# Weights of the modulation first, zero products on TensorE, values in pairs, and another order of the last batch

## What is computed

```
mod = swish(c) @ w_mod + b_mod
sh_msa, sc_msa, g_msa, sh_mlp, sc_mlp, g_mlp = split(mod, 6)
xn = ln(x) * (1 + sc_msa) + sh_msa
q, k, v = heads(xn @ w_qkv + b_qkv)
q, k = ln(q, g_q), ln(k, g_k)
o = softmax(q @ k.T * HD ** -0.5) @ v
x = x + g_msa * (o @ w_proj + b_proj)
xn2 = ln(x) * (1 + sc_mlp) + sh_mlp
x = x + g_mlp * (gelu(xn2 @ w1 + b1) @ w2 + b2)
```

## Time and profile before

| what | value |
|---|---|
| median of 3 runs | 204.37 us (201.6 to 204.68) |
| the profiled execution's own time | 202.29 us |
| its span, first to last instruction | 200.5 us |
| mean granted clock of PE in it | 0.974 |
| PE busy | 166.0 us, 83% |
| DVE busy | 125.7 us, 63% |
| ACT busy | 108.9 us, 54% |
| POOL busy | 65.5 us, 33% |

### The profile page before, as it was taken

One profiled execution on the slowest core, in us unless ns is written; L12 is line 12 of the kernel. 1 busy time (PEld: TensorE's weight loads), 2 busy tenths in 40 slices (PEclk: granted clock), 3 DMA queues, 4 the chain that ended last, 5 costly groups with the idle time before them and its releaser, 6 DMA issues.

```text
span 200.5 us, 3873 instructions
## 1 busy us (share of the span) xinstructions
PE 166.0 (83%) x1504; PEld 93.9 (47%) x1504; DVE 125.7 (63%) x312; ACT 108.9 (54%) x146; POOL 65.5 (33%) x81
## 2 busy tenths in 40 slices
PE   0009982749979999999999999899659999999983
PEld 0005131413434454544644545344316796979773
DVE  3269568819548587679677774955856786564212
ACT  2001024255998879978888799976842404132320
POOL 8103513067418146173290201600462352220000
PEclk9999999999999999999999999999856999999999
DMA  0993028950000000000000000000000000101101
GB/s 10 247 211 120 5 51 251 399 158 0 3 2 0 3 3 0 0 3 0 3 0 5 0 3 2 0 3 0 3 0 0 0 3 0 60 3 59 59 0 59
DMA packets 4535, 8.67 MB, mean 43 GB/s; under 512 B 821, under 2 KB 3071, under 8 KB 4406
## 3 DMA queue, kind: packets, MB, share of 16 engines
q1 hardware_dynamic: 4228, 8.41, 14.0%
q10 hardware_dynamic: 288, 0.01, 0.1%
HBM read 7.21 MB, written 1.21 MB: 42 GB/s over the span
## 4 chain that ended last, share of the span: by engine, by line
PE 73%; DVE 9%; DMA 6%; ACT 3%; POOL 3%; issue 3%; SPq 1%; POOLq 0%; ACTq 0%
PE ps_o L1103 15%; PE ps_o L1226 10%; PE ps_s L1209 9%; PE ps_s L1088 8%; PE ps_x L1022 8%; DMA pTs<-in_b_mod 6%; PE ps_x L1029 4%; PE ps_o L1131 4%; PE ps_x L1113 4%; PE ps_s L1006 3%; PE ps_o L1015 3%; PE ps_x L1197 2%; PE ps_s L1000 2%; POOL z2s L464 2%; DVE kst L753 2%
## 5 line engine op out<-in xcount | busy, mean ns | idle before, releaser
L552 ACT ACTIVATE pTs<-ps_s,escale 128x1024 f32<-128x1024 f32 x64 | 68.9, 1109 | 17.1 <-PE ps_s L1088 16.1
L1103 PE MATMUL ps_o<-pTs,v 128*32 128x256 f32 x512 | 42.9, 410 | 5.0 <-ACT raw L523 2.5
L609 ACT ACTIVATE late<-ps_s 120x512 f32<-120x512 f32 (+1 forms) x20 | 11.9, 596 | 26.1 <-PE ps_s L1209 26.1
L1088 PE MATMUL ps_s<-qT,kT 32*128 32x256 f16 x256 | 24.3, 282 | 1.0 <-DVE qT L777 1.0
L1226 PE MATMUL ps_o<-w_sb,late 120*128 120x144 f32 (+1 forms) x160 | 20.7, 287 | 0.7 <-ACT late L609 0.7
L1226 PEld LDWEIGHTS ps_o<-w_sb,late 120*128 120x128 f32 (+1 forms) x160 | 19.9, 190 | 1.2 <-ACT late L609 1.2
L1209 PE MATMUL ps_s<-late,w1s 110*120 110x512 f16 (+1 forms) x80 | 18.8, 386 | 0.0
L1103 PEld LDWEIGHTS ps_o<-pTs,v 128*32 128x32 f32 x512 | 10.5, 110 | 17.5 <-ACT pTs L552 7.1
L1088 PEld LDWEIGHTS ps_s<-qT,kT 32*128 32x128 f16 x256 | 7.1, 93 | 24.4 <-issue 20.8
L464 POOL TENSOR_TENSOR z2s<-z2s,mbc 128x576 f32<-128x576 f32 x4 | 8.4, 2092 | 28.7 <-DVE z2s L901 28.7
L397 POOL COPY v<-raw 128x288 f32<-128x288 f32 x8 | 4.0, 496 | 41.8 <-DVE ssum L726 34.9
(11 more groups left out here) (115 smaller groups left out, 263.4 us busy)
## 6 DMA issues: line engine op xcount, KB each, us to landing
mbc<-mod_rows SPq DMA_DIRECT2D x6, 432.0 KB, 7.4
late<-in_w SPq DMA_DIRECT2D x1, 990.0 KB
xall<-in_x SPq DMA_DIRECT2D x1, 864.0 KB, 13.6
out<-late SPq DMA_DIRECT2D x3, 288.0 KB, 2.3
z2s<-in_w_qkv SPq DMA_DIRECT2D x1, 742.5 KB
mbc<-mod_rows SPq DMA_DIRECT2D x2, 288.0 KB, 6.4
pTs<-in_w_mod SPq DMA_DIRECT2D x1, 486.0 KB
w_sb<-in_w SPq DMA_DIRECT2D x1, 337.5 KB
```

What stands on the lines that cost most here:

```text
L552: nc.scalar.activation(pT[u % NP].rearrange("p g n -> p (g n)"), ps_s[:, 2 * (u % 2):2 * (u % 2) + 2, :].rearrange("p a n -> p (a n)"), AC ...
L609: nc.scalar.activation(hT[k % 2][0:FW[f], f, :], ps_s[0:FW[f], (NF * k + f) % 4, :], ACT.Gelu_apprx_tanh, scale=UNSCALE).then_inc(gelued, 1)
L1088: mm = nc.tensor.matmul(ps_s[:, 2 * (u % 2) + a, half * N:(half + 1) * N], kT[par][rows, j, i * P:(i + 1) * P], qT[par][rows, j, :], start ...
L1103: mm = nc.tensor.matmul(ps_o[SLOT * g:SLOT * (g + 1), 1, (j % 2) * N:(j % 2 + 1) * N], v[par][:, i, h, :], pT[u % NP][:, g, :], start=(i = ...
```

## The change

In the start SP loads `w_mod` and `b_mod` ahead of `w_qkv` and x, and the rest of x is issued only when the first x has landed. PE gets a buffer of zeros, `idle_z`, and multiplies it with itself, 128 by 128 by 512 in fp16, into a bank that isn't in use: 17 times before it waits for `w_mod`, 38 times before it waits for `wq`, and 2, 10 and 8 times within the preparation of batch 0. Their results are overwritten. DVE makes the constants of g first; the standardising and first modulating of batch 0 come before `wq`, in `xt`. `scores` 1 of batch 0 comes before `make_qkv(1)`.

In the loop PE takes values 0 and 1, 2 and 3, 4 and 5 in a row, each pair behind one more unit of scores. POOL splits w1 after batch 1's share, DVE in two halves at the end of batches 3 and 4.

The statistics' roots of batches 0 to 3 (tiles 0 to 7, `READY`) are taken in batch 6, so that the first pair's z is made there. In the last batch the z transposes of pair 0 and 1 go by halves through a bank of `ps_o`, the hidden products of pair 0 begin before values 7, and those of pair 1 before the output products of pair 0.

```diff
...
+        def z_bank(k, h):
+            return (x_bank if k < 2 else bank16(h)).rearrange("p c n -> p (c n)").rearrange("p (c n) -> p c n", c=2)
...
             xp = x.rearrange("b (p i) c -> p b (i c)", i=I)
-            sp.dma_start(xall[:, 0:2], xp[:, 0:2]).then_inc(ld_x, 16)
+            sp.dma_start(wm_sb[0:HT], w_mod).then_inc(ld_wm, 16)
+            sp.dma_start(wm_sb[HT:HT + 1, 0, :], b_mod.rearrange("(o c) -> o c", o=1)).then_inc(ld_wm, 16)
             sp.dma_start(wq_f, w_qkv).then_inc(ld_wq, 16)
             sp.dma_start(lo_row[:], lo_rows).then_inc(ld_wq, 16)
-            sp.dma_start(wm_sb[0:HT], w_mod).then_inc(ld_wm, 16)
-            sp.dma_start(wm_sb[HT:HT + 1, 0, :], b_mod.rearrange("(o c) -> o c", o=1)).then_inc(ld_wm, 16)
+            sp.dma_start(xall[:, 0:2], xp[:, 0:2]).then_inc(ld_x, 16)
             sp.dma_start(id32[:], ident).then_inc(ld_id, 16)
+            sp.wait_ge(ld_x, 16)
             sp.dma_start(xall[:, 2:B], xp[:, 2:B]).then_inc(ld_rest, 16)
...
+            pool.wait_ge(ld_w1, 16)
+            nc.gpsimd.tensor_scalar(w1_h, w1_f, WS, lo_row[:, 0:1], ALU.mult, ALU.mult).then_inc(w1_made, 1)
...
-            pool.wait_ge(ld_w1, 16)
-            nc.gpsimd.tensor_scalar(w1_h, w1_f, WS, lo_row[:, 0:1], ALU.mult, ALU.mult).then_inc(w1_made, 1)
...
-            x_roots(first_stats)
...
+            x_roots(first_stats)
...
                 exponentials(n, 3)
-                if not makes:
-                    early_roots()
+                if n == B - 2:
+                    early_roots(0, slice(0, READY))
                 exponentials(n, 4)
...
                 exponentials(n, 6)
+                if not makes:
+                    early_roots(1, slice(READY, EARLY))
                 exponentials(n, 7)
...
-            output(B - 1, 1, 1)
...
+                    if (k, f) == (0, 2):
+                        output(B - 1, 1, 1)
...
+            dve.wait_ge(ld_wq, 32)
+            wh = wq_f[:, :, 0:2 * H].rearrange("p c (h d) -> p c h d", d=HD)
+            nc.vector.tensor_reduce(wq_m[:], wh, AX.X, ALU.add).then_inc(D.sem, 1)
+            dve.wait_ge(ld_x, 16)
+            x_stats(first_stats)
+            x_aggregate(first_stats)
+            done("mean")
+            nc.vector.scalar_tensor_tensor(wh, wq_m[:].unsqueeze(3).broadcast_to([KR, NC, 2 * NH, HD]), -1.0 / HD, wh,
+                                           ALU.mult, ALU.add).then_inc(D.sem, 1)
+            x_newton(first_stats)
...
+            dve.wait_ge(first_stats.root.sem, first_stats.root.after(0, "rstd"))
+            for i in range(I):
+                nc.vector.tensor_scalar(xt[:, i, :], xi[:, i, :], mv[:, i, 0:1], rstd[:, i:i + 1],
+                                        ALU.subtract, ALU.mult).then_inc(prep.mx.sem, 1)
+            dve.wait_ge(set_act.sem, set_act.after(0, "A01"))
+            dve.wait_ge(prep.mx.sem, prep.mx.after(0, "z1"))
+            nc.vector.tensor_tensor(xt[:], xt[:], mb(0, A1), ALU.mult).then_inc(prep.mx.sem, 1)
+            def shift_first():
+                dve.wait_ge(prep.mx.sem, prep.mx.after(0, "za"))
+                nc.vector.tensor_tensor(xm[:], xt[:], mb(0, B1), ALU.add).then_inc(prep.mx.sem, 1)
...
+            def zT_half(k, h):
+                dve.wait_ge(ln2_pe.sem, ln2_pe.after(k, f"zT{h}"))
+                if k >= 2:
...
+                nc.vector.tensor_copy(zT[k % 2][:, 2 * h:2 * h + 2, :], z_bank(k, h)[0:KR]).then_inc(ln2_T.sem, 1)
+            def zT_out(k):
+                for h in range(2):
+                    zT_half(k, h)
...
+            def roots(part, tiles):
+                if part < 2:
+                    dve.wait_ge(root_act.sem, root_act.after(part, "y0"))
...
+            def first_half_z():
+                roots(0, ready)
+                standardise2(0)
+            def w1_half(c):
+                dve.wait_ge(w1_made, 1)
+                nc.vector.scalar_tensor_tensor(w1s[:, c:c + 2], w1_f[:, c:c + 2], WS, w1_h[:, c:c + 2],
+                                               ALU.mult, ALU.subtract).then_inc(w1_made, 1)
...
+                if n == B - 2:
+                    aggregate(ready)
...
                     xT_out(n + 2, prep)
+                if n == B - 2:
+                    first_half_z()
                 if n >= 2:
                     residual(n - 2)
+                if n in (3, 4):
+                    w1_half(2 * (n - 3))
...
                                             ).then_inc(fin_dve.sem, 1)
-            early, late_tiles = range(EARLY), range(EARLY, B * I)
             projected(B - 3)
             normalise(B - 2)
+            stack2(0)
             residual(B - 3)
+            channels(B - 2)
+            zT_half(0, 0)
+            standardise2(1)
+            zT_half(0, 1)
+            dve.wait_ge(w1_made, 3)
+            nc.vector.memset(hT[1][FW[-1]:FW[-1] + 1, NF - 1, :], 1.0).then_inc(h_ones, 1)
+            projected(B - 2)
             aggregate(early)
-            dve.wait_ge(root_act.sem, root_act.after(0, "y0"))
-            roots(0, early)
-            standardise2(0)
-            channels(B - 2)
-            dve.wait_ge(w1_made, 1)
-            nc.vector.scalar_tensor_tensor(w1s[:], w1_f, WS, w1_h, ALU.mult, ALU.subtract).then_inc(w1_made, 1)
-            projected(B - 2)
-            stack2(0)
+            stack2(1)
+            roots(1, early)
             residual(B - 2)
-            zT_out(0)
-            standardise2(1)
+            zT_half(1, 0)
+            zT_half(1, 1)
+            standardise2(2)
             normalise(B - 1)
-            stack2(1)
             channels(B - 1)
-            standardise2(2)
+            stack2(2)
             projected(B - 1)
             residual(B - 1)
-            dve.wait_ge(w1_made, 2)
-            nc.vector.memset(hT[1][FW[-1]:FW[-1] + 1, NF - 1, :], 1.0).then_inc(h_ones, 1)
-            zT_out(1)
-            stack2(2)
             aggregate(late_tiles)
             dve.wait_ge(root_pool, 2)
-            roots(1, late_tiles)
+            roots(2, late_tiles)
+            standardise2(3)
             final(0)
             zT_out(2)
-            standardise2(3)
             stack2(3)
             final(1)
             zT_out(3)
...
+            def keep_busy(count):
+                for _ in range(count):
+                    nc.tensor.matmul(ps_x[:, 0, :], idle_z[:, 0:P], idle_z[:], start=True, stop=True)
+            pe.wait_ge(idle_set, 1)
+            keep_busy(17)
...
             mm.then_inc(set_pe.sem, 1)
+            keep_busy(38)
             pe.wait_ge(set_dve.sem, set_dve.after(0, "wq"))
...
                 pe.wait_ge(gen_dve.sem, gen_dve.after(B - 1, "lo"))
             transpose_x(0, prep)
+            keep_busy(2)
             make_qkv(0, prep)
+            qkv_used(0, prep)
+            keep_busy(10)
             transpose_x(1, prep)
-            qkv_used(0, prep)
+            keep_busy(8)
             transpose_k(0, prep)
             transpose_q(0, prep)
...
                     qkv_used(n + 1, prep)
                 if not first:
                     transpose_o(n - 1, 1 - par)
-                values(n, 0, par)
                 if ahead:
                     if n >= 2:
                         pe.wait_ge(gated, n - 1)
                     transpose_x(n + 2, prep)
+                scores(n, 3, par)
+                values(n, 0, par)
                 values(n, 1, par)
-                scores(n, 3, par)
-                values(n, 2, par)
                 scores(n, 4, par)
                 if not first:
                     transpose_o_tok(n - 1)
+                scores(n, 5, par)
+                values(n, 2, par)
                 values(n, 3, par)
-                scores(n, 5, par)
                 if makes:
                     transpose_k(n + 1, prep)
-                values(n, 4, par)
                 scores(n, 6, par)
                 if makes:
                     if not first:
                         pe.wait_ge(post_dve.sem, post_dve.after(n - 1, "och"))
                     transpose_q(n + 1, prep)
+                scores(n, 7, par)
+                values(n, 4, par)
                 values(n, 5, par)
-                scores(n, 7, par)
                 if makes:
                     scores(n + 1, 0, 1 - par)
                 values(n, 6, par)
...
             scores(0, 0, 0)
+            scores(0, 1, 0)
             make_qkv(1, prep)
...
+            def transpose_z_half(k, h):
...
+                if k < 2 and (k or h):
+                    pe.wait_ge(ln2_T.sem, ln2_T.after(k, f"zT{h}") - 1)
+                if k > 2:
+                    pe.wait_ge(ln2_T.sem, ln2_T.after(k - 1, f"zT{h}"))
...
-                    if k:
-                        pe.wait_ge(ln2_T.sem, ln2_T.after(k - 1, f"zT{h}"))
...
+                    transpose_z_half(k, h)
...
+                    if m == 0:
+                        pe.wait_ge(exped, B * U - 1)
...
             transpose_o_tok(n - 1)
             values(n, 3, par)
             scores(n, 5, par)
```

(29 more changed lines are left out.)

119 lines of the change are left out of this document (48 added, 71 removed).

## The result

| | before | changed kernel |
|---|---|---|
| time, median | 203.38 us (4 runs, 201.6 to 204.68) | 190.25 us (4 runs, 189.51 to 191.37) |
| ratio to before, 95% interval | | 0.9387, 0.928 to 0.9493 |
| profiled execution: time, span | 202.29, 200.5 | 189.51, 187.7 |

The change is faster by 6.1%; 191.0 us had been said, with 187 to 197 as the range. A second series on another chip gave 190.48 us (189.88 to 190.69, 5 runs) beside 203.1 for before, ratio 0.9444 (0.9403 to 0.9486). Some runs of before fell into a slower state of the chip and the ratios leave them out, so a ratio isn't always the quotient of the two medians.

A forecast was written before the change was run, and what follows sets the result against it. PE was taken to bound the kernel, with 73% of the chain. Savings of 4.6, 1.0, 0.4, 0.8 and 5.4 made 12.2 us, span 188.3, with 1.8 around it 190.1; 191.0 was said, range 187 to 197.

The forecast's parts named there:

- the sum: Whole kernel: savings of 4.6, 1.0, 0.4, 0.8 and 5.4 make 12.2 us, span 188.3.
- rival 1: Start: zero products don't raise the clock, so the kernel ends slower, +8.5 us, 211; chance 0.06.
- the signs: What would show the forecast, among them first transposes between 22 and 23 us and a loop batch of 13.0.
- PE is the later one: Start: `xst` is ready at 21.4 to 21.6 us, PE reaches the first transposes only at 22.3.
- I take the middle: Batch 0: -1.0 us, bounds 0 and -2, between a clock that holds and one that falls in PE's 3.8 us wait.
- the prediction's warm end: Batch 0: ends at 15.8 us from its first scores with warm work, 17.9 if the clock falls.
- Rival 3: ACT doesn't hold PE in the loop and batch 0 comes warm: 187 to 189 us; chance 0.1.
- the late root: Last batch: ACT's root (0.55 us) starts at 13.0, exponential 7 ends at 14.8, and PE waits 1.4.
- rival 2: Clock rises but falls again at L1006 or a wait, in the start or before exponential 7: 193 to 198; chance 0.27.

The follow-up runs named there:

- the second one: The changed kernel unchanged, run a second time and profiled: median 190.48 us, span 188.7.
- the swap on ACT: Changed kernel with ACT doing exponential 5 before the copy `oT` in every batch: median 189.42 us, ratio 0.9235 to before.
- the aggregation ahead of the copy: Changed kernel with DVE's aggregate of batches 4 and 5 moved ahead of the second zT copy: median 189.53 us, ratio 0.9264 to before.
- all three edits: Changed kernel with exponential 5 before copy `oT`, aggregation before the second zT copy, and 20 zero products in batch 0's wait: 187.79 us, ratio 0.9249 to before.

## Why the prediction was right, and where it was not

The mechanisms that the sum names did come, but that the total is only 0.6 us of span off is partly luck: the start brought 0.7 more than said, the loop 0.4 and batch 6 0.25, and batch 0 brought 0.8 less.

**The start: more than predicted (-5.3, not -4.6), and PE was not the late one.** The clock did rise: L1038 took 3.07 us where L1006 took 5.86, and `make_qkv(0)` 1.63. That settles rival 1. The sum had `w_mod` at 9 us, and it was there by 7.2 (without zero products L1030 starts at 7.21), near the lower of its two ends; PE was through with the 38 zero products at 20.7, not 22.3. Then it waited 1.03 us for `xst` at 21.75, a little before the 22 to 23 that the signs gave. So the failing step is "PE is the later one". The DVE chain behind `lo_row` was put at 9.2 us; it took 10.3 (11.38 to 21.70). What was missing is that standardising does not run beside `wq_h`. DVE in order of time, and POOL beside it:

```profile
15.34 0.16 DVE L1329 SCALAR_TENSOR_TENSOR nt<-mv,nt 128x4 f32<-128x4 f32 x1
15.54 1.55 DVE L1331 SCALAR_TENSOR_TENSOR rstd<-nt,y 128x4 f32<-128x4 f32 x1
...
15.35 1.74 POOL L410 TENSOR_SCALAR wq_h<-z2s,lo_row 110x1728 f16<-110x1728 f32 x1 [9.58 <-DVE z2s L685]
```

An operation on 128x4 takes 1.55 us and ends at 17.09, exactly with POOL's. So the 1.2 us of standardising and modulating come after it and before `wq`. The Trainium skill, "SBUF — State Buffer", "Who interferes with whom", says that a DVE operation with two SBUF inputs and a GpSimd operation that reads SBUF exclude each other for a whole instruction. The traces agree, and the kernel before has a second case: there `gabs` is the operation with two inputs behind the start of `wq_h` (15.32 to 17.03 in the earlier trace rows). DVE of before, then `gabs` in the changed kernel:

```profile
10.94 0.16 DVE L1280 SCALAR_TENSOR_TENSOR rstd<-nt,y 128x4 f32<-128x4 f32 x1
...
15.56 1.48 DVE L680 TENSOR_TENSOR gabs<-gp,gneg 128x9 f32<-128x9 f32 x1
```

```profile
7.40 0.17 DVE L663 TENSOR_TENSOR gabs<-gp,gneg 128x9 f32<-128x9 f32 x1
```

Each of the two operations takes 0.16 or 0.17 us where POOL does nothing, and about 1.5 where it is issued within 0.3 us behind `wq_h`'s start; both then end with `wq_h`. No kernel moves `wq_h` alone, so what the stretched operation costs the start isn't measured by itself.

**Batch 0: -0.2, not -1.0.** "I take the middle" between a clock that holds and one that falls was the mistake: here it fell, and what that costs depends on how long it stays low. The transposes came 7.06 us after the first scores, not 6.4; PE stood 4.48 us, not 3.8; the clock fell. A clock that holds is worth 1.4 us against this profile (14.02 against 15.46) and 2.45 against the second one (16.47); the prediction's distance between its two ends was 2.1. With the clock held, batch 0 takes 16.1 us where the prediction's warm end was 15.8.

**The loop: -0.8, not -0.4.** The mechanism was right, also in size: a wait of 0.29 for ACT before scores 7 (0.34 predicted), 9.20 us into the batch (9.27 predicted), and a batch of 12.97 (13.05 predicted). Each batch came 0.08 under the sum, and five of them are the difference. Rival 3's half, that ACT doesn't hold PE, is refuted by the swap on ACT: the gain of 0.36 per batch was waiting behind ACT.

**Batch 6: -1.05, not -0.8.** ACT was expected to end the batch at 11.3 us; it took 11.0, with PE busy 10.59 (10.6 predicted). The bound on ACT was put 0.3 too high. The prediction names POOL's moved conversion first, and that brings 0.4 of the 1.05; the other 0.65 is the new order, as the kernels with the old one show (11.65).

**The last part: -5.4 as predicted.** From 126.30 to PE's last product it takes 58.2 us, and 58.1 had been said, but two misses cancel in it: PE is busy 55.4 (54.7 predicted) and stands 2.8 (3.4 predicted). Exponential 7 waited for the late root, 1.04 us (1.4 predicted), and the aggregation ahead of the copy takes that wait away. No low clock after 120 us, as predicted; with the last batch in the old order it is back. So rival 2 didn't come in the start or in the last batch. Its mechanism did come in batch 0, where the sum carried it as the middle of two ends and not as a case of its own. The prediction gave the whole 5.4 to this part without saying which edit brings it: the order brings 3.2, much of it perhaps by the clock, and the other 2.2 go to the early split of w1 by subtraction.

## What to carry to other kernels

A wait of PE costs a second time where the clock falls behind it, so it is worth filling with products on zero data into a bank that is free, also in the middle of a kernel and not only at its start: 20 such products brought 1.4 us or more. That they also make the times of one kernel agree better isn't shown: kernels with them spread over 0.2, 0.25, 1.45 and 1.8 us, others over 0.4 to 2.6. Where two edits cure the same late operand, measure each alone: -4.0 and -3.4 made -5.3. When a loop is freed by swapping two operations of a helper engine, look at the peeled last round by itself: the same swap that saved 0.36 us in each round cost a wait of 1.2 us there, and in one of two kernels a low clock behind it.

## What the runs showed of the hardware that was not expected

- Products on zeros do hold and raise the granted clock. In the changed kernel it is at its full level by 7.3 us, behind 17 products of 128x128 weights and 512 columns. Ten microseconds of unbroken fp32 products with 73 rows of weights (4.21 and 5.93 us) left it at the low level in the kernel without zero products: `make_qkv` after it still took 3.06 us.
- The row of the granted clock is 1.00 in that stretch, as it is for the first 48 us in the earlier trace rows. The level at the start of an execution has to be read from durations.
- With the same wait of 4.48 us the clock was low for 3.4 us in one execution of the changed kernel and for 6.8 in another, and for 13.65 in the kernel with the loop's old order, whose PE waits 1.93 and 1.82 us there with one unit of values between. A wait of 1.20 us for `oT` in the last batch was followed by a low clock with all three edits (133.3 to 136.8) and by none in the kernel with the swap alone. What decides this stays open.
- A DVE operation of 0.16 us that reads two SBUF operands takes 1.48 to 1.56 us behind POOL's conversion of 110x1728, and ends with it, in before, in the changed kernel and in all their variants.
